# Layer 1's attention: preparation, routing and picking placed anew within each group of eight units

## What is computed

```
x = x + tanh(g_xattn[0]) * cross_attention0(layernorm(x), ctx)     # 8 heads of 64
x = x + tanh(g_ffn[0])   * experts0(layernorm(x))                  # top 2 of 8, SiLU-gated
q = (layernorm(x) @ Wq + bq), k = (ctx @ Wk + bk), v = (ctx @ Wv + bv)   # layer 1: 16 heads of 8
x = x + tanh(g_xattn[1]) * (softmax(q k^T / sqrt(8)) v @ Wo + bo)
logits = layernorm(x) @ router.T; vals, idx = top_k(logits, 2)     # layer 1's experts, GELU
x = x + tanh(g_ffn[1])   * sum(softmax(vals) * expert(idx))
```

## Time and profile before

| | us |
|---|---|
| median of 3 runs | 753.79 (753.32 to 755.35) |
| the profiled execution | 752.22 |
| its span | 750.5 |
| PE busy in the span | 629.7 (84%) |
| DVE busy | 557.5 (74%) |
| POOL busy | 448.3 (60%) |
| ACT busy | 444.4 (59%) |
| layer 1's attention, first to last score product | about 382 to 609 |

### The profile page before, as it was taken

The page is one execution under the profiler, slowest core; times in us unless marked ns, Lnnn a source line. Parts: engine busy times, 40 slices in busy tenths (PEclk is TensorE's granted clock), DMA queues, the critical chain, the costliest instruction groups (busy, mean ns, idle before and its releaser), DMA issues.

```text
span 750.5 us, 16523 instructions
## 1 busy us (share of the span) xinstructions
PE 629.7 (84%) x4501; PEld 571.5 (76%) x4501; DVE 557.5 (74%) x1971; ACT 444.4 (59%) x1275; POOL 448.3 (60%) x665
## 2 busy tenths in 40 slices
PE   6889787878776869998778998898879986799997
PEld 4668687868766869898767787787877876689885
DVE  3368688787876797997887888988868765455784
ACT  2477676766634546665657686677665742344462
POOL 4034347776766877886563435677656763766761
PEclk9599999999977899999989999999989995799999
DMA  9446667544523335335534533625414003333555
GB/s 258 132 116 163 179 169 201 140 115 129 146 76 93 93 102 154 104 101 156 146 100 102 126 96 70 137 78 103 120 34 117 25 28 87 101 93 100 148 167 162
DMA packets 127383, 89.48 MB, mean 119 GB/s; under 512 B 30996, under 2 KB 116276, under 8 KB 127260
## 3 DMA queue, kind: packets, MB, share of 16 engines
q1 hardware_dynamic: 110844, 64.93, 34.1%
q0 software_dynamic: 8128, 17.65, 7.2%
q10 hardware_dynamic: 8320, 5.85, 2.8%
HBM read 50.73 MB, written 39.85 MB: 121 GB/s over the span
## 4 chain that ended last, share of the span: by engine, by line
PE 37%; DVE 27%; ACT 13%; issue 10%; POOL 6%; DMA 4%; SPq 3%; DVEq 1%; ACTq 0%; POOLq 0%
PE banks L1162 8%; PE banks L1181 5%; PE banks L1025 4%; DVE row_max L1418 3%; POOL x_rows L1905 3%; PE banks L905 2%; SPq L815 2%; ACT prob L1294 2%; PE banks L968 2%; DVE prob L1421 2%; DVE x_res L1754 2%; PE banks L1010 2%; DMA v_rows<-vo 2%; ACT xm L1287 2%; POOL y_rows L1912 1%
## 5 line engine op out<-in xcount | busy, mean ns | idle before, releaser
L1912 POOL DMA_INDIRECT y_rows<-y_sb,result_at x134 | 131.0, 978 | 61.6 <-issue 24.6
L1162 PE MATMUL banks<-xb,up 128*128 128x128 f32 x820 | 123.4, 290 | 22.5 <-DVE hidden L1730 11.4
L1905 POOL DMA_INDIRECT x_rows<-xm,row x120 | 120.4, 1003 | 32.5 <-issue 27.5
L1162 PEld LDWEIGHTS banks<-xb,up 128*128 128x128 f32 x820 | 110.5, 203 | 32.7 <-issue 14.2
L1867 POOL TENSOR_TENSOR v_flat<-v_raw,row_head 104x64 f32<-104x64 f32 (+1 forms) x128 | 55.8, 464 | 73.1 <-ACT v_raw L1335 72.7
L1319 ACT ACTIVATE prob_t<-banks 128x512 f32<-128x512 f32 x192 | 73.3, 439 | 27.6 <-PE banks L992 27.6
L1025 PE MATMUL banks<-v_flat,prob_t 128*128 128x108 f32 (+2 forms) x640 | 86.9, 285 | 2.6 <-issue 1.7
L1025 PEld LDWEIGHTS banks<-v_flat,prob_t 128*128 128x128 f32 (+1 forms) x640 | 80.6, 199 | 9.6 <-ACT prob_t L1319 5.8
L1181 PE MATMUL banks<-down,hidden 128*128 x536 | 84.9, 283 | 0.1
L1833 POOL TENSOR_TENSOR prob<-prob,inv_sum 128x616 f32<-128x616 f32 x32 | 39.1, 1221 | 58.7 <-DVE inv_sum L1481 58.6
L1181 PEld LDWEIGHTS banks<-down,hidden 128*128 128x128 f32 x536 | 73.6, 199 | 0.5 <-issue 0.5
(11 more groups left out here) (238 smaller groups left out, 1630.4 us busy)
## 6 DMA issues: line engine op xcount, KB each, us to landing
vo_flat<-v_rows SPq DMA_DIRECT2D x32, 256.0 KB
x_norm<-x_rows SPq DMA_DIRECT2D x74, 72.0 KB
v_rows<-vo SPq DMA_DIRECT2D x38, 128.0 KB
x_far<-x_rows SPq DMA_DIRECT2D x60, 72.0 KB
gathered<-y_rows ACTq DMA_DIRECT2D x32, 128.0 KB
q_rows<-up_raw SPq DMA_DIRECT2D x8, 512.0 KB, 2.8
q_even<-q_rows SPq DMA_DIRECT2D x12, 256.0 KB
q_odd<-q_rows SPq DMA_DIRECT2D x12, 256.0 KB
```

What stands on the lines that cost most here:

```text
L1162: done = pe.matmul(banks[:, UP_BANK[i % 2], part * P:(part + 1) * P], block_w[:, i % WR, part // 2, part % 2 * P:(part % 2 + 1) * P], xb[: ...
L1905: pool.indirect_dma_start(out=x_rows[layer][:, :], out_offset=bass.IndirectOffsetOnAxis(ap=row[:, n, c:c + 1], axis=0), in_=xm[:, i % 2, j ...
L1912: pool.indirect_dma_start(out=y_rows[layer][:, :], out_offset=bass.IndirectOffsetOnAxis(ap=result_at[:, i % (2 * YR):i % (2 * YR) + 1], ax ...
```

## The change

In every group from the fourth on (g >= 3) the preparation is moved within the eight units: norm from place 1 to 0, normalize from 2 to 1, k1 from 4 to 2, xt from 7 to 3, q1 from place 0 of the next eight to place 5. In layer 1's routing mturn goes from place 0 to 7 (one unit earlier), route from 2 to 1, pick from 3 to 2. What pick did after its two copies (comparisons, picked, group_sum, counts) is a task of its own, `count`, which stays at place 3. Rank, lead, scatters and loads stay. Group 6's routing stays as it was, and so does, in order, all of layer 0 and what is dealt out during the expert stages, where pick and count stand side by side. No arithmetic is added or taken away.

```diff
@@ -123,11 +123,10 @@
     at = {}
-    usual = steps[0]
     for g in range(NG):
         u = spacing * g + lag
-        steps_of = steps[g - NG + 4] if NG - 3 <= g < NG - 1 else usual
-        for kind, step in zip(("mnorm", "mnormalize", "mturn", "route", "pick", "rank", "lead"), steps_of[0]):
+        steps_of = steps[g]
+        for kind, step in zip(("mnorm", "mnormalize", "mturn", "route", "pick", "count", "rank", "lead"), steps_of[0]):
             if g >= ROUTED[layer] and kind == "rank":
                 continue
@@ -267,11 +266,8 @@
     for g in range(2, NG):
         u = 2 * GS * (g - 2)
-        put(u + 1, ("norm", NG + g))
-        put(u + (2 if g > 2 else 4), ("normalize", NG + g))
-        put(u + (4 if g > 2 else 6), ("k1", g))
-        put(u + 7, ("xt", NG + g))
-        put(u + 8, ("q1", g))
+        for kind, step in zip((("norm", NG + g), ("normalize", NG + g), ("k1", g), ("xt", NG + g), ("q1", g)), (0, 1, 2, 3, 5) if g > 2 else (1, 4, 6, 7, 8)):
+            put(u + step, kind)
         put(u + 9, ("q_load", g))
@@ -338,7 +334,7 @@
             step.append(late.pop(0))
-            if late and late[0] == ("expert_w",):
+            if late and late[0][0] in ("count", "expert_w"):
                 step.append(late.pop(0))
@@ -359,9 +355,11 @@
-    tasks = [route_tasks(0, GS, 6, ((range(7), (5, 6, 7, 8)), (range(7), (5, 6, 7, 8)), ((0, 1, 2, 3, 3, 4, 5), (5, 5, 5, 5)))),
-             route_tasks(1, 2 * GS, 13, (((0, 1, 3, 5, 6, 7, 9), (9, 11, 13, 15)), ((0, 1, 3, 5, 6, 7, 9), (8, 9, 10, 11)),
-                                         ((0, 1, 2, 3, 4, 5, 6), (6, 6, 7, 7))))]
+    tight = ((0, 1, 2, 3, 4, 4, 5, 6), (5, 6, 7, 8))
+    steps0 = [tight] * 6 + [((0, 1, 2, 3, 3, 3, 4, 5), (5, 5, 5, 5)), tight]
+    spread1 = (0, 1, 2, 4, 5, 6, 7, 9)
+    steps1 = [(spread1, (9, 11, 13, 15))] * 5 + [(spread1, (8, 9, 10, 11)), ((0, 1, 2, 3, 4, 4, 5, 6), (6, 6, 7, 7)), (spread1, (9, 11, 13, 15))]
+    tasks = [route_tasks(0, GS, 6, steps0), route_tasks(1, 2 * GS, 13, steps1)]
@@ -1559,6 +1557,12 @@
                         dve.tensor_copy(xm[:, s, :, D + 1], top_idf[:, s, :, 0]).then_inc(sem("xm_place"))
+                elif kind == "count":
+                    layer, g = t[1:]
+                    i = layer * NG + g
+                    s = i % 2
+                    w.wait_ge("top_idx", (GS + 1) * (i + 1))
+                    w.wait_ge("constants", N_CONSTANTS)
                     iota3 = iota8[:, :].unsqueeze(1).to_broadcast([P, GS, NEXP])
@@ -1874,7 +1878,7 @@
-                elif kind == "pick" and t[1] == 0:
+                elif kind == "count" and t[1] == 0:
```

## The result

The changed kernel takes 771.36 us (median of 6 runs) against 753.56 for the kernel before in the same comparison; the ratio is 1.0223, 95% interval 1.017 to 1.0276. It is slower, by some 17 us. The profiled execution took 769.98 us, with a span of 768.2.

What follows compares the result with a forecast made beforehand. DVE's work plus its holes was taken to bound each group. Holes +3.6 and copies -0.9 gave +2.7 us per full group, +11 for four, +11.7 with the other units: 765.5 us against the median of 753.79, range 756 to 774.

Steps and rivals of the forecast that it cites:

- What bounds the kernel: Units 24 to 31: DVE bounds; the group's 29.26 us is 26.4 us of DVE's work plus 2.9 us of holes.
- without work at place 2: Place 2: k1's products stand ahead of `project`, so DVE's residual update waits about 0.3 us (bounds 0 and 1.07).
- New hole at place 1: Route waits for the `rows1` bank until ACT's row copy behind normalize's activations; DVE waits 3.7 us (floor 3.0, ceiling 4.2).
- Hole at place 7: Mturn replaces xt but waits for the last `v_raw` copy; unit as long as before, DVE's hole grows from 1.8 to 2.5 us.
- Hole at place 0: q1's products leave and norm enters ahead of the residual update; place 0 becomes 4.0 us with no hole, -1.1 us.
- Copies: Pick's cast and two copies at place 2, away from POOL's multiplications: about 0.2 us apiece, booked at -0.9 us.
- The other groups: Units 8 to 15: +1.3 us (bounds 0 and 2); units 48 to 55: 0; units 56 to 60: -0.6.
- Sum: Full group: holes +3.6, copies -0.9, together +2.7 us, 29.3 to 32.0; four groups +11, whole +11.7 us.
- (c): Rival, chance 0.13: PE's pauses lower its clock in two to five groups, 2.1 us each, giving 770 to 776 us.
- Around the pause PE is dense: Argument against the clock falling at place 1's new hole, where PE was expected idle for some 1.9 us.
- unit 47 could keep its clock: Unit 47, before at granted clock 0.51, could keep its clock with q1's products now in unit 45: 2 us less.

## Why the prediction was right, and what it sized too small

**What bounds the kernel.** The account by DVE's work and holes held. In the group with full clock the two holes were 3.54 and 2.54 us, against 3.7 and 2.5 in the prediction, and DVE had 0.2 us without work at place 2, against 0.3.

**New hole at place 1.** Right in mechanism and size: place 2's maxima come at 3.97 + 5.75 = 9.72 us, 9.85 was predicted. That the bank is its cause was shown by the run that changes the bank alone (5.75 to 3.63 us). That normalize adds 1.5 us to it was shown by the run that moves normalize (to 4.23).

**Hole at place 7.** 4.16 to 4.18 us for the unit, 4.1 predicted; DVE's wait 2.54, and L1432 no longer waits there.

**Hole at place 0.** Removed: the unit takes 3.97, predicted 4.0.

**Copies.** 0.17 us each in place of 0.61, 0.46 and 0.49, together 1.05 us less, 0.9 predicted. DVE's busy time in the group fell by only 0.77, because `picked` at place 3 takes 0.42 us instead of 0.19 beside POOL. The rule of the Trainium skill ("SBUF — State Buffer", "SBUF: two separate sides"), that a DVE copy and a GpSimd instruction exclude each other, agrees with rows 6. Its part about DMA issue did not show: three copies of 0.17 us inside a scatter issue of 0.96.

**The other groups.** Units 8 to 15 grew by 1.5 (1.3 predicted), 48 to 55 by 0.3 (0), units 56 to 62 shrank by 1.7 (0.6 predicted for 56 to 60).

**Sum.** The forecast for a full group was 32.0 us and +2.7, against 31.73 and +2.5 measured with the full clock. The step that failed is how the cases were joined: the fall of the clock was put as a rival (c) of 0.13, though it adds to the forecast rather than replacing it. Its row had been read: 0.51 after a pause of 2.70 us. "Around the pause PE is dense" was the judgement that failed: in unit 17 PE was busy for 2.13 of the 4 us ahead of the router products. The clock fell behind that pause in three of the four full groups. By the difference to the run with 17 turnings this cost 3.2, 1.6 and 3.2 us in the profiled executions, unit 47 left out; (c) had 2.1 us each. In the medians the change is 17.8 us, of which 0.9% or some 7 us go with PE's pauses filled. So 765.5 was 6 us short, and the measured 771.4 lies where (c) put it, 770 to 776. The range reached far enough to hold (c) in part, and that is what caught the 6 us, not the sum. The direction and the forecast's own terms held: without these falls the four groups grew by 2.3, 2.5, 2.8 and 2.2 us, where 2.7 was summed. That unit 47 could keep its clock, with q1 moved to unit 45, did not come: it took 6.00 us at a mean clock of 0.57, as against 6.15 before.

The Trainium skill ("TensorE: Matmul & The Clock Gate", section on the HAM clock gate) has idle stretches throttle the engine; the filled pauses agree, with a ratio of 1.016 with over half of the pause filled and 1.0127 with all of it, against 1.0223.

**Not settled.** Why units 24 to 31 of the changed kernel kept the clock with a pause of 1.91 us, while units 16 to 23 lost it with 2.00 and units 32 to 47 with 1.91, was not tried. PE's busy time ahead of it doesn't tell them apart (2.05 of 4 us where the clock stayed, 2.13 where it fell). Nor was it tried what makes places 0 and 1 take 8.82 us with the routing moved alone.

## What to carry to other kernels

A task in a hand-written order also takes its place in the life of the buffer or bank that it uses: before moving one, ask who used that bank last in the new order, what that user's reader has queued ahead of it, and who is queued behind the wait. When an engine gets a new pause, price the pause and, apart from it, the work done at the lower clock after it; add them, don't weigh them as alternatives. And a small copy on one engine can cost three times its length beside a neighbour's long instruction, so where it stands may matter more than how many there are. When you move it out of the way, look at what takes its place there: the comparisons that did lost half of the gain again.

## What the runs showed of the hardware that was not expected

- Adding PE work made a kernel faster: 17 turnings in each of six units took it from 1.0223 to 1.0127 of the kernel before. The granted clock stayed at 1.00 in units 17 and 18, where it had been at 0.56 and 0.50 from 449 us on, and DVE's wait in unit 25 was unchanged at 3.54 us.
- PE's clock fell behind a wait for a busy DVE too: 4.29 of 4.5 us busy on DVE, 2.71 on PE, a pause of 1.87 us, and a granted clock of 0.56 in the 3.5 us after. That the pause was the cause was not tested there.
- DVE's casts and copies of 128x8 and 128x4 took 0.17 us in the midst of a scatter issue on POOL, and 0.46 to 0.61 beside POOL's multiplication. DVE's comparisons and `picked` were slower beside POOL as well, 0.64 and 0.38 us against 0.28 and 0.19.
